# Two-layer graph attention on one core: the second weighing partly on ScalarE, and both low parts of the f32 turns at the head of VectorE's loop period

## The chip, the cores and the metric

The program runs on one core of a Trainium2 chip. The metric is the device time of one execution in microseconds (us), the median of several; lower is better. The profile is one execution recorded by the hardware profiler. Its engines are TensorE (PE, and PEld for its weight loads), VectorE (DVE), ScalarE (ACT), GpSimd (POOL) and SyncE (SP), which here only issues DMAs.

## The reference

Two graph-attention layers run over 4096 nodes with 128 features and one 4096 x 4096 adjacency matrix, f32 throughout:

```
h = relu(layernorm(x));  q, k, v = h@Wq.T+bq, h@Wk.T+bk, h@Wv.T+bv
x = x + elu(softmax(where(adj > 0, q@k.T/sqrt(128), -9e15)) @ v)          # layer 1
g = relu(layernorm(x));  t = g@W;  s1 = t@a[:128];  s2 = t@a[128:]
e = where(adj > 0, leaky_relu(s1[:,None] + s2[None,:], 0.01), -9e15)
x = x + t + softmax(e) @ g                                                # layer 2
```

## The kernel before

Both layers go through the nodes in 32 strips of 128 query rows. `T` is 32, `NC` is 8 chunks of four tiles of 128.

**Layer 1, the loop.** `all_periods` gives every engine 32 periods, one for each strip `s`; the middle 24 are a hardware loop of four periods a turn. The order on each engine is the order of the code, and engines meet only in counted semaphores. In period `s`:

- PE turns the last quarter of the exponentials of strip `s` in f32 (`turn`, i = 0 and 1), and in between computes scores of strips `s+1` and `s+2` (`make_scores`, 6 matmuls of 512 columns for each part `k` of 1024 columns). The rest is turned in bf16 (`turn_high`) and multiplied with v (`times_v`).
- ACT copies the two f32 turns out as bf16 high parts (`copy_pT`: tiles `pT_high0`, `pT_high1`), copies the next q strip, copies the sums and the bf16 turns (`copy_hiT`), takes the exponentials of strip `s+1` (`exps`, after the maximum of that strip) and ends with the elu of strip `s-1` (`elu_exp`).
- DVE makes the low parts of the f32 turns (`turned_low`, i = 0 and 1: f32 in PSUM minus the bf16 high part), the low parts of the exponentials in SBUF (`low_part`, k = 0, 1, 2), which SP then turns by DMA (`lowT`), adds the mask and takes the running maximum of strip `s+1` and `s+2` (`add_mask`, k = 0 to 3) and reduces it (`find_max`).
- POOL finishes the elu (`add_elu`, three small instructions), makes the additive mask of strip `s+2` (`make_mask`, L365, two halves), adds the halves of the sums (`add_halves`, two small ones) and turns the adjacency of strip `s+3` into bytes (`make_bytes`, L360, two halves).

`make_scores(s+2, 0)` overwrites the PSUM tile that `add_mask(s+1, 2)` reads, and so waits for it; `make_scores(s+2, 1)` waits for `add_mask(s+1, 3)` in the same way.

**The edge.** After the loop the rows are normalised, turned, and multiplied with `wa`. The features are weighed twice by exponentials of `s2`: `weigh(c)` writes `v1[0]`, and `weigh_words(c, 1)` writes `v1[1]`, chunk by chunk (L344). POOL splits each weighed chunk into two bf16 halves in place (`split_words`, L340). PE computes `t = g@W` with `hw_product(c)` in four PSUM tiles that `hw_add` empties. ACT writes sign bytes of strips 0 to 3 for each key tile (`sign_bytes`, L308; `EARLY` is strips 0 and 1, `LATE` strips 2 and 3). This block of code ends in a meeting of all five engines; each then loads a flag from memory (L1364) and branches to the fast way.

**Layer 2.** In the fast way DVE first computes exponents (L1437 to L1441), then weighs the chunks of `v1[1]` that are left, then makes the masks of strips 1, 2, 3 (`cut`, three instructions each: L323, L327, L332), then compares 12 key tiles for the next four strips, and then takes results and cuts by turns. PE sums strip after strip, 64 matmuls each (L1664): 32 key tiles with `v1[0]`, then 32 with `v1[1]`. In strip 0 each chunk of `v1[1]` beyond the early ones waits for POOL's split. Strip `s` waits for the mask `parts_ready` of `cut`. Four strips further the masks need the signs that ACT writes meanwhile.

`LOW_EARLY` is the number of chunks of `v1[1]` weighed ahead of the meeting, `LATE_EARLY` the number of key tiles whose `LATE` signs ACT writes ahead of it.

## Time and profile before

| | |
|---|---|
| median of three runs | 746.63 us (746.05 to 747.23) |
| the profiled execution | 748.01 us, of which its span 746.2 us |
| loop of layer 1, from the second f32 turn group to the last | about 78 to 451 us of the span |
| edge, from there to the first matmul of strip 1 in layer 2 | 451 to 516 us |
| layer 2 | 516 to 741 us, then the last result |
| busy share of the span | PE 96%, PEld 81%, DVE 76%, ACT 72%, POOL 61% |
| mean granted TensorE clock | 0.986 of full speed |

A timeline row gives the start in us of the span, the duration, the engine, the line, the operation and its tiles, the number of instructions merged into it, and in brackets the engine's idle time ahead of it with what ended it. Durations of neighbours on one engine overlap by some 0.1 us, so the distance between two starts is what an instruction costs. A windows row gives the stretch, its length, the busy time of each engine with its number of instructions, the granted clock, the DMA share and the GB/s. Spans on POOL are rough.

### The profile page before, as it was taken

Reading aid. Unit: us, or ns where it says so; the run is one execution under the profiler, and the core shown is the slowest. Engines: PE = TensorE matmul, PEld = TensorE weight load, DVE = VectorE, ACT = ScalarE, POOL = GpSimd, SP = SyncE. Lnnn points to the kernel's source line nnn. Section 1 sums busy time; section 2 is a strip of 40 time slices with the busy share of each in tenths; the row PEclk is TensorE's granted clock in tenths of the full one; section 3 lists DMA queues with packets and bytes.
Section 4 is the critical chain, followed back from the end, with each engine's and each line's share of the span. In section 5 each row is a group of like instructions: output and inputs, shape, how many; then the busy total and the mean of one; then the engine's idle time right before and its main releaser. Section 6 shows DMA issues by size and latency. Waiting matters only on the chain. (4 is left out here: it accounts for less than half of the span.)

```text
span 746.2 us, 18361 instructions
## 1 busy us (share of the span) xinstructions
PE 714.8 (96%) x6269; PEld 603.7 (81%) x6269; DVE 567.5 (76%) x1203; ACT 539.8 (72%) x1083; POOL 452.9 (61%) x388
## 2 busy tenths in 40 slices
PE   7988999999999999999999999967999999999997
PEld 5667888888888888888888878855888888888885
DVE  5977787787878878788787887779978477577572
ACT  4755877778777787777877778869597797887810
POOL 5688799999999999999999998664000000000000
PEclk9999999999999999999999999978999999999999
DMA  7179999998988989889798863994333343442200
GB/s 240 64 257 300 251 275 240 267 249 245 276 243 265 253 248 274 240 269 255 247 271 238 275 135 82 176 85 85 87 77 76 81 96 66 94 95 63 40 11 13
DMA packets 192784, 132.51 MB, mean 178 GB/s; under 512 B 173537, under 2 KB 180193, under 8 KB 184545
## 3 DMA queue, kind: packets, MB, share of 16 engines
q1 hardware_dynamic: 192000, 131.63, 66.4%
q8 instruction: 28, 0.46, 0.3%
q10 hardware_dynamic: 576, 0.26, 0.1%
q14 instruction: 20, 0.16, 0.1%
q0 software_dynamic: 160, 0.00, 0.0%
HBM read 71.04 MB, written 18.89 MB: 121 GB/s over the span
## 5 line engine op out<-in xcount | busy, mean ns | idle before, releaser
L797 ACT ACTIVATE scores<-scores,neg_max 128x1024 f32<-128x1024 f32 x128 | 146.1, 1143 | 45.3 <-DVE neg_max L928 45.3
L941 DVE TENSOR_TENSOR low<-scores 128x1024 bf16<-128x1024 f32 x96 | 135.6, 1412 | 38.5 <-ACT scores L797 38.4
L1210 PE MATMUL spare<-v_parts,hiT 128*128 128x256 bf16 x768 | 161.6, 274 | 0.0
L922 DVE CUSTOM_DVE_ANT_0 scores<-ps_s,mask_both 128x1024 f32<-128x1024 f32 x128 | 155.9, 1218 | 0.7 <-POOL mask_both L365 0.4
L365 POOL TENSOR_SCALAR mask_both<-mask_bytes 128x2048 bf16<-128x2048 uint8 x64 | 151.7, 2371 | 5.4 <-POOL mask_bytes L360 0.4
L360 POOL TENSOR_SCALAR mask_bytes<-adj_both 128x2048 uint8<-128x2048 int32 x64 | 148.5, 2338 | 3.8 <-DMA adj_both<-in_adj 3.0
L1206 PE MATMUL spare<-v_parts,lowT 128*128 128x128 bf16 x768 | 144.5, 220 | 4.3 <-DMA lowT<-low 4.3
L811 ACT ACTIVATE hiT<-spare 128x512 bf16<-128x512 bf16 (+1 forms) x128 | 102.5, 802 | 35.3 <-PE spare L1180 32.8
L1664 PE MATMUL ps_x<-q_parts,over_k 128*128 128x258 bf16 x1024 | 118.5, 276 | 5.5 <-POOL q_parts L340 2.5
L1664 PEld LDWEIGHTS ps_x<-q_parts,over_k 128*128 128x128 fp8e4 x1024 | 99.8, 99 | 22.7 <-POOL q_parts L340 3.3
L1145 PE MATMUL ps_s<-k_hi,q_strip 128*128 128x512 f32 x256 | 111.8, 437 | 2.4 <-PEq L83 1.9
L1146 PE MATMUL ps_s<-k_lo,q_strip 128*128 128x512 f32 x256 | 100.8, 394 | 0.0
L1147 PE MATMUL ps_s<-k_hi,q_strip 128*128 128x512 f32 x256 | 100.8, 394 | 0.0
L1210 PEld LDWEIGHTS spare<-v_parts,hiT 128*128 128x128 bf16 x768 | 75.5, 98 | 8.3
L1206 PEld LDWEIGHTS spare<-v_parts,lowT 128*128 128x128 bf16 x768 | 75.5, 98 | 7.6 <-issue 3.5
L308 ACT ACTIVATE v_parts<-s_block,s_col 128x512 fp8e4<-128x512 f32 x116 | 72.2, 717 | 0.0
L1592 ACT ACTIVATE sums<-ps_x,ac 128x258 f32<-128x258 f32 x63 | 26.3, 470 | 62.4 <-PE ps_x L1664 62.4
L1159 PE MATMUL spare<-ident,scores 128*128 128x128 f32 x256 | 69.4, 275 | 0.9 <-ACT hiT L811 0.9
L934 DVE TENSOR_TENSOR pT_low<-spare,pT_high 128x512 bf16<-128x512 f32 x64 | 43.9, 688 | 31.9 <-ACT pT_high L804 31.9
L1180 PEld LDWEIGHTS spare<-ident_half,scores 128*128 128x128 bf16 x768 | 46.3, 98 | 25.3 <-issue 23.8
L1180 PE MATMUL spare<-ident_half,scores 128*128 128x128 bf16 x768 | 64.8, 220 | 0.0
L1664 PE MATMUL ps_x<-q_parts,v_parts 128*128 128x258 bf16 x512 | 59.8, 273 | 0.0
(179 smaller groups left out, 1302.1 us busy)
## 6 DMA issues: line engine op xcount, KB each, us to landing
adj_both<-in_adj SPq DMA_DIRECT2D x64, 1024.0 KB, 5.3
mask_bytes_dram<-mask_bytes SPq DMA_DIRECT2D x32, 512.0 KB, 2.8
x_sb<-in_x SPq DMA_DIRECT2D x8, 256.0 KB, 8.4
out<-res SPq DMA_DIRECT2D x32, 64.0 KB, 1.6
lowT<-low SPq DMA_TRANSPOSE x96, 4.7
mask_both<-s_row_dram SPq DMA_DIRECT2D x2, 768.0 KB, 7.3
over_k<-mask_bytes_dram SPq DMA_TRANSPOSE x16, 4.6
scores<-mask_bytes_dram SPq DMA_TRANSPOSE x16, 4.6
```

The lines of the kernel that those rows point to most:

```text
L360: return nc.gpsimd.tensor_scalar(mask_bytes[par][:, half(h)], adj_sb[h], 1.0, 0.0, ALU.min, ALU.max)
L365: return nc.gpsimd.tensor_scalar(out, src, -NEG, NEG, ALU.mult, ALU.add)
L797: nc.scalar.activation(sc, sc, ACT.Exp, bias=neg_max[:, bn:bn + 1], accum_out=row_sum[:, bn, k:k + 1]).then_inc(exp_done, 1)
L811: nc.scalar.activation(hiT[k][:, half_of], ps_t[(2 + u) % 3][:].bitcast(BF16)[:, half_of], ACT.Copy).then_inc(hiT_ready, 1)
L922: nc.vector.tensor_tensor_reduce(out=scores[bn % 2][:, part(k)], in0=ps_s[k % 2][:], in1=mask[bn % 2][:, part(k)], scale=1.0, scalar=LOWES ...
L941: nc.vector.tensor_tensor(low[k][:], p, high_half(p), ALU.subtract).then_inc(low_done, 1)
L1145: nc.tensor.matmul(o, high, k_hi[:, col], start=True, stop=False)
L1146: nc.tensor.matmul(o, high, k_lo[:, col], start=False, stop=False)
L1180: last = nc.tensor.transpose(out[:, D * t:D * t + D], high[:, D * t:D * t + D], ident_half[:])
L1206: return nc.tensor.matmul(ps_a[:, 0, :], rest, v_parts[:, t, 0, :], start=False, stop=False)
L1210: last = nc.tensor.matmul(ps_a[:], high, v_parts[:, t, :, :], start=first, stop=final)
L1664: last = nc.tensor.matmul(ps_x[b % 2][k][:], by_key_tile(m, t)[:, b], v1[k][:, t, :].bitcast(BF16), start=(t == 0), stop=(t == T - 1))
```

## The change

In each loop period but the first and the last, `turned_low(s, 1)` stands right behind `turned_low(s, 0)`, ahead of `low_part(s, b, 1)` and `add_mask(s + 1, bn, 2)`. At the edge the chunks 2 to 5 of `v1[1]` are weighed by ACT ahead of the meeting, 16 activations of one tile each, and POOL splits them there, behind everything else that it does in this block. DVE weighs only chunks 0 and 1 ahead of the meeting, as before, and 6 and 7 behind it. ACT writes the `LATE` signs of 2 key tiles ahead of the meeting where it wrote 6, and of 22 behind it where it wrote 26; DVE writes those of the last 8 tiles between the masks of strips 1 and 2. PE computes `hw_product(4)` and `(5)` one place earlier each.

```diff
             EARLY = slice(0, 2)
             FIRST, MIDDLE, LAST = slice(0, 24), slice(24, 30), slice(30, 32)
-            LOW_EARLY = 2
+            LOW_EARLY = 6
+            LOW_VECTOR = 2
+            VECTOR_LATE = 8
             LATE = slice(2, 4)
-            LATE_EARLY = 6
+            LATE_EARLY = 2
...
                         if c == NC - 2:
-                            for n in range(LOW_EARLY):
+                            for n in range(LOW_VECTOR):
                                 pool.wait_ge(low_weighed, n + 1)
                                 split_words(pool, n, 1)
+                    for c in range(LOW_VECTOR, LOW_EARLY):
+                        pool.wait_ge(low_by_scalar, c - LOW_VECTOR + 1)
+                        split_words(pool, c, 1)
...
                     nc.scalar.activation(s1_row[:, 512:1024], ps_s3[1], ACT.Copy).then_inc(s1_out, 1)
+                    for c in range(LOW_VECTOR, LOW_EARLY):
+                        for t in range(4 * c, 4 * c + 4):
+                            last = nc.scalar.activation(v1[1][:, t, 0:D], h_sb[:, t, :], ACT.Relu, scale=v1[1][:, t, D:D + 1])
+                        last.then_inc(low_by_scalar, 1)
                     for t in range(LATE_EARLY):
                         sign_bytes(0, s1_row, t, LATE)
...
                             turned_low(s, 0)
+                            turned_low(s, 1)
                             low_part(s, b, 1)
                             add_mask(s + 1, bn, 2)
-                            turned_low(s, 1)
                             low_part(s, b, 2)
...
-                    for c in range(LOW_EARLY):
+                    for c in range(LOW_VECTOR):
                         weigh_words(c, 1).then_inc(low_weighed, 1)
...
                     s1_product(1, ps_s3[1])
+                    hw_product(4)
                     pe.wait_ge(top_ready, 1)
...
-                    hw_product(4)
+                    hw_product(5)
                     pe.wait_ge(top_d, 1)
...
-                    for c in range(5, NC):
+                    for c in range(6, NC):
                         hw_product(c)
...
                             if isinstance(g, int) and g == 0 and b == 2:
                                 dve.wait_ge(late_signs, 1)
+                                dve.wait_ge(vector_late, 1)
...
                         cut(0, 0, 1)
+                        for t in range(T - VECTOR_LATE, T):
+                            last = compare_bytes(nc.vector, 0, s1_row, t, LATE)
+                        last.then_inc(vector_late, 1)
                         cut(0, 0, 2)
...
-                        for t in range(LATE_EARLY, T):
+                        for t in range(LATE_EARLY, T - VECTOR_LATE):
                             last = sign_bytes(0, s1_row, t, LATE)
```

On DVE, in a period of the loop of layer 1: `pT_low0` and `pT_low1` are the low parts of the two f32 turns, `low1` and `low2` those of two parts of the exponentials, `scores1<-ps_s0` the masked scores. Before:

```order
L934 TENSOR_TENSOR pT_low0<-spare0,pT_high0 128x512
L941 TENSOR_TENSOR low1<-scores0 128x1024
L921 MEMSET gate 128x1
L922 ISA scores1,row_max<-ps_s0,mask_both 128x1024
L922 ISA row_max 128x1
L934 TENSOR_TENSOR pT_low1<-spare1,pT_high1 128x512
L941 TENSOR_TENSOR low2<-scores0 128x1024
```

And of the change, the same stretch:

```order
L943 TENSOR_TENSOR pT_low0<-spare0,pT_high0 128x512
L943 TENSOR_TENSOR pT_low1<-spare1,pT_high1 128x512
L950 TENSOR_TENSOR low1<-scores0 128x1024
L930 MEMSET gate 128x1
L931 ISA scores1,row_max<-ps_s0,mask_both 128x1024
L931 ISA row_max 128x1
L950 TENSOR_TENSOR low2<-scores0 128x1024
```

`low1` and the masked scores of part 2 now stand behind the second f32 turn; everything from `low2` on has its old place.

On DVE, behind the meeting, at the head of layer 2: `q_parts` is `v1[1]`, `over_k` the masks of strips 1 to 3, `v_parts` the next ones. Before:

```order
L344 SCALAR_TENSOR_TENSOR q_parts<-adj_both,q_parts 128x4x128 x6
L323 TENSOR_SCALAR over_k<-over_k 128x1024
L327 SCALAR_TENSOR_TENSOR over_k<-over_k 128x1024
L332 TENSOR_TENSOR over_k<-over_k 128x1024
L323 TENSOR_SCALAR over_k<-over_k 128x1024
```

And of the change:

```order
L344 SCALAR_TENSOR_TENSOR q_parts<-adj_both,q_parts 128x4x128 x2
L323 TENSOR_SCALAR over_k<-over_k 128x1024
L327 SCALAR_TENSOR_TENSOR over_k<-over_k 128x1024
L332 TENSOR_TENSOR over_k<-over_k 128x1024
L313 TENSOR_SCALAR over_k<-mask_both,s_col 128x2x128 x8
L323 TENSOR_SCALAR over_k<-over_k 128x1024
```

Four of six weighings are gone ahead of the mask of strip 1, and eight comparisons stand between it and the mask of strip 2.

On POOL, on both sides of the meeting (the branches and the load of the flag), where `q_parts` is split. Before:

```order
L340 TENSOR_TENSOR q_parts<-q_parts 128x516 x10
L573 UNCONDITIONAL_BRANCH
L1418 UNCONDITIONAL_BRANCH
L1364 TENSOR_LOAD flag
L1364 ISA x2
L1365 COMPARE_AND_BRANCH
L340 TENSOR_TENSOR q_parts<-q_parts 128x516 x6
```

And of the change:

```order
L340 TENSOR_TENSOR q_parts<-q_parts 128x516 x14
L575 UNCONDITIONAL_BRANCH
L1428 UNCONDITIONAL_BRANCH
L1374 TENSOR_LOAD flag
L1374 ISA x2
L1375 COMPARE_AND_BRANCH
L340 TENSOR_TENSOR q_parts<-q_parts 128x516 x2
```

Four splits have moved from behind the meeting to ahead of it.

## Rows read from the trace of the kernel before

**Rows 1.** Windows: the loop of layer 1.

```profile
78.47:451.30 372.83, 369.05 (x3362) 311.68 (x3361) 299.02 (x588) 283.57 (x561) 349.92 (x260) 1.00 0.87 249
```

**Rows 2.** Timeline of POOL, from one period's `add_halves` to the next one's.

```profile
313.69 0.46 POOL L710 TENSOR_TENSOR acc_sb<-acc_sb 128x128 f32<-128x128 f32 x1
...
321.24 5.64 POOL L365 TENSOR_SCALAR mask_both<-mask_bytes 128x2048 bf16<-128x2048 uint8 x2
...
326.96 0.46 POOL L710 TENSOR_TENSOR acc_sb<-acc_sb 128x128 f32<-128x128 f32 x1
```

**Rows 3.** Timeline of POOL in the period that begins at 438.19.

```profile
440.55 1.54 POOL L721 TENSOR_TENSOR x_sb<-x_sb,att_exp 128x128 f32<-128x128 f32 x1
442.17 4.73 POOL L365 TENSOR_SCALAR mask_both<-mask_bytes 128x2048 bf16<-128x2048 uint8 x2
```

**Rows 4.** Timeline of DVE: a low part beside rows 2, then the same period as rows 3.

```profile
320.79 1.44 DVE L941 TENSOR_TENSOR low<-scores 128x1024 bf16<-128x1024 f32 x1
...
440.56 1.22 DVE L941 TENSOR_TENSOR low<-scores 128x1024 bf16<-128x1024 f32 x1
...
443.44 1.70 DVE L941 TENSOR_TENSOR low<-scores 128x1024 bf16<-128x1024 f32 x1
...
446.33 0.16 DVE L928 TENSOR_REDUCE neg_max<-row_max 128x1 f32<-128x4 f32 x1
```

**Rows 5.** Timeline of ACT in the same period and the next.

```profile
438.89 0.30 ACT L825 ACTIVATE att_pos<-att 128x128 f32<-128x128 f32 x1
...
439.32 0.60 ACT L804 ACTIVATE pT_high<-spare 128x512 bf16<-128x512 f32 x1
...
441.82 0.60 ACT L804 ACTIVATE pT_high<-spare 128x512 bf16<-128x512 f32 x1 [1.50 <-PE spare L1159]
...
446.52 1.15 ACT L797 ACTIVATE scores<-scores,neg_max 128x1024 f32<-128x1024 f32 x1 [0.55 <-DVE neg_max L928]
...
452.62 0.58 ACT L804 ACTIVATE pT_high<-spare 128x512 bf16<-128x512 f32 x1
454.93 0.60 ACT L804 ACTIVATE pT_high<-spare 128x512 bf16<-128x512 f32 x1 [1.72 <-PE spare L1159]
```

**Rows 6.** Timeline of PE: first matmul of `make_scores(s+2, 0)` in that period.

```profile
445.32 0.48 PE L1145 MATMUL ps_s<-k_hi,q_strip 128*128 128x512 f32 x1
```

**Rows 7.** The chain that ended last, from the head of layer 2.

```profile
504.54 7.02 DVE q_parts L344 x6
...
516.31 52.22 PE ps_x L1664 x448
...
568.53 7.18 PE ps_x L1664 x64
```

**Rows 8.** Timeline of POOL: the last splits ahead of the meeting, and those behind it.

```profile
496.68 1.05 POOL L340 TENSOR_TENSOR q_parts<-q_parts 128x516 bf16<-128x516 f32 x1 [0.76 <-DVE q_parts L344]
505.22 8.70 POOL L340 TENSOR_TENSOR q_parts<-q_parts 128x516 bf16<-128x516 f32 x6 [7.49 <-DVE q_parts L344]
```

**Rows 9.** Timeline of PE at the edge.

```profile
489.70 0.39 PE L1269 MATMUL ps_s<-v_parts,ident_half 128*128 128x256 bf16 x1 [1.16 <-ACT scores L869]
...
499.01 3.40 PE L1280 MATMUL spare<-w_next,scores 128*128 128x128 f32 x24
503.81 5.54 PE L1664 MATMUL ps_x<-q_parts,over_k 128*128 128x258 bf16 x48 [1.40 <-issue]
```

**Rows 10.** Windows of 1 us at the edge; the clock is the third figure from the end.

```profile
489.00:490.00 1.00, 0.29 (x3) 0.30 (x4) 1.00 (x2) 1.00 (x8) 1.00 (x2) 0.87 1.27 288
...
520.00:521.00 1.00, 1.00 (x9) 0.80 (x8) 0.96 (x2) 1.00 (x2) 0.00 (x0) 0.77 0.00 0
```

**Rows 11.** Timeline of ACT: late signs ahead of the meeting and behind it.

```profile
495.07 2.57 ACT L308 ACTIVATE over_k<-mask_both,s_col 128x256 fp8e4<-128x256 f32 x6
504.86 10.49 ACT L308 ACTIVATE over_k<-mask_both,s_col 128x256 fp8e4<-128x256 f32 x26
```

**Rows 12.** Timeline of DVE: the twelve comparisons of layer 2.

```profile
522.48 4.84 DVE L313 TENSOR_SCALAR v_parts<-mask_both,s_col 128x512 uint8<-128x512 f32 x12
```

4 lines of the change are left out of this document (2 added, 2 removed).

## The prediction

> **What bounds the kernel now.** I read the profile in three steps: the windows of the loop, the timelines of the four engines within one of its periods, and then the chain that ended last with the timelines around the meeting.
>
> In the loop PE is busy for 369.05 of 372.83 us, and the clock is full [rows 1]. The stretch is 28 periods, so one takes 13.315 us on average. PE alone would need (369.05 / 28 =) 13.18, and what is missing, 3.78 us over all periods, is the most that any reordering in the loop can win. POOL explains most of it: from one `add_halves` to the next it takes (326.96 - 313.69 =) 13.27 us, with nothing but back-to-back work between [rows 2]. In that time it is held up once, by a `low_part` of DVE: the two halves of L365 take 5.64 us there [rows 2] and 4.73 in another period [rows 3]; in that other period it is the small L721 that starts with `low1` and takes 1.54 [rows 3, 4], where the small L710 takes 0.46 [rows 2]. So POOL loses 0.9 us or a little more to DVE in each period, and without that would need (13.27 - 0.91 =) 12.36.
>
> At the edge the chain runs through DVE. Behind the meeting it weighs six chunks in 7.02 us and makes the mask of strip 1, and only at 516.31 can PE begin strip 1 [rows 7]. From 516.31 on the chain is PE without a gap, at 7.18 us for 64 matmuls [rows 7]: layer 2 is bound by PE, and whatever moves the start of strip 1 moves the end. The first 448 matmuls take 52.22 us where 7 x 7.18 = 50.26 are normal, since the clock, which fell to half in the stalls of strip 0, is full again only in the window from 520 [rows 7, 10]. The effective start of a full-speed layer 2 is 516.31 + 1.96 = 518.27.
>
> **The loop.** No instruction is added or taken away. `pT_low1` moves ahead of `low1`, and since it needs ACT's second copy, DVE now waits for it before `low1`. In the period shown the first copy starts at 439.32, the second at 441.82 after an idle time of 1.50 [rows 5], so ACT could start it 1.00 after the first, and PE makes it wait. From the second copy `P` on I add up three cycles.
>
> First, ACT and DVE. Copy and its low part 1.24 (439.32 to 440.56, as for the first copy), of which `pT_low1` is about 0.6; `low1` and the mask of part 2 2.28 (440.56 to 443.44, less 0.60 for the `pT_low1` between); `low2` to the maximum 2.89 (443.44 to 446.33) [rows 4, 5]. `low2` takes 1.70 and `low1` 1.22 [rows 4], so 0.48 of the 2.89 is a wait, and 2.41 stays without it. Maximum to exponential 0.19, exponentials, copies and elu to the next first copy 6.10 (446.52 to 452.62), first copy to second 1.00 [rows 4, 5]. The sum is 1.24 + 2.28 + 2.41 + 0.19 + 6.10 + 1.00 = 13.22, or 13.70 with the wait.
>
> Second, PE and DVE. The mask of part 2 now ends at P + 1.24 + 2.28 = P + 3.52; in the period shown that is 445.34, and PE starts the scores that need it at 445.32 [rows 5, 6]. So this wait just closes. From there to the next second copy PE takes 454.93 - 445.32 = 9.61 [rows 5, 6]. The cycle is 13.13, and with an estimated 0.05 for the semaphore 13.18.
>
> Third, POOL: 12.36 if no low part holds it. `low1` will start at the first copy + 1.00 + 1.24 = + 2.24. The first half of L365 starts, without L721's hold of (1.54 - 0.46 =) 1.08, at 442.17 - 1.08 - 439.32 = + 1.77 [rows 2, 3, 5]. So `low1` comes 0.47 after it, which the trace doesn't show. Two cases bound it. L365 that starts 0.45 after a low part (321.24 against 320.79) costs POOL 0.91 and the low part 0.2 [rows 2, 4]. `low2` that starts 1.27 after L365 (443.44 against 442.17) is held 0.48 and POOL nothing [rows 3, 4]: the first half lets go 1.75 after its start, and the second half, which starts at 442.17 + 2.36 = 444.53 while `low2` still works until 445.06, isn't delayed, so that a half has no need of the port in its first 0.53 us. By that `low1` comes just in time to be first, by 0.06. It then holds POOL; if POOL becomes slower than the 13.22 of ACT by this, L365 slides later against `low1`, and the hold shrinks. I take POOL as held, with 13.27 as now, since the nearest case with POOL held costs what it loses now. The 28 periods then take what they take: **0 for the loop**, within -1.5 (28 x 0.05, period 13.22) and +2 us. The cover of this edit is thin: the mask of part 2 had ended some 2.5 us before PE needed it (443.44 - 0.60 against 445.32), and will end as it is needed.
>
> The Trainium skill, page "SBUF — State Buffer", section "Who interferes with whom", says that a VectorE instruction with two SBUF inputs and a GpSimd instruction that reads SBUF exclude each other, whichever starts first keeping the port pair for its whole length. Here the row differs: `low2`, which starts 1.10 before the end of the first L365 half, is held for 0.48 only [rows 3, 4]. By the page `low1` would be held for 2.36 - 0.47 = 1.9, and the rival below would be the likeliest case.
>
> **The edge, up to the meeting.** ACT's 16 activations cost 0.30 each at most [rows 5], 4.8 us from 495.07 on [rows 11], plus two signs at 2.57 / 6 = 0.43; it is done by 500.7 even so, and hidden by PE, which ends at 499.01 + 3.40 = 502.41 [rows 9]. PE has one product less at its end and fills a stall with it: some 1.1 us earlier, 501.3. POOL becomes the last. It ends now at 496.68 + 1.05 = 497.73, and gets four more splits. Each takes 1.05 alone and 8.70 / 6 = 1.45 beside DVE's weighing [rows 8]. That is 501.9 to 503.5, and since DVE works there on two instructions with two inputs of about the same length, I take 503.4. Behind the meeting PE starts 1.40 after the last engine's end [rows 9]: at **504.8**, 1.0 later than now.
>
> **The edge, behind it.** DVE starts weighing at 504.54 + 1.0 = 505.5, takes two chunks of 1.17 (7.02 / 6), and then as now 4.75 (511.56 to 516.31) for the mask of strip 1 [rows 7]: ready at 512.6 at the latest. PE's strip 0 no longer waits for splits: 504.8 + 7.2 = 512.0. But PE was idle from 501.3 to 504.8. An idle time of 1.40 at this meeting left the clock alone, one of 1.16 ahead of 489.70 was followed by its fall in the window from 489 [rows 9, 10]; 3.5 us will bring it down. It came back 4.2 us after PE's steady work began at 516.31, with a loss of 1.96 [rows 7, 10]. I take the same loss: strip 0 ends at 512.0 + 2.0 = 514.0, with its mask ready, and from there on the clock is full. The gain is 518.27 - 514.0 = **4.3 us**.
>
> What else moved is hidden. The eight comparisons cost less than 4.84 / 12 = 0.40 each [rows 12], 3.2 in all, up to 515.8; the 22 signs at 10.49 / 26 = 0.40 [rows 11] are done by 505.9 + 8.9 = 514.8; two more masks at most by 521. PE needs the mask of strip 2 at 521.2. ACT begins the next signs, those of strips 4 to 7, half a microsecond earlier than now (514.8 against 504.86 + 10.49 = 515.35 [rows 11]), and PE needs them 4.3 us earlier, at 514.0 + 3 x 7.18 = 535.5, 20.7 us after ACT begins; in the trace PE meets no wait there [rows 7], and I take it as hidden still. Were it not, at most (4.3 - 0.5 =) 3.8 us would come back.
>
> **The sum.** The profiled execution took 748.01 with a span of 746.2; the median of the runs is 746.63, 1.38 less. Against its own time: 748.01 + 0 - 4.3 = 743.7; against the median **742.3**.
>
> **The rivals.**
>
> *The edge gives more.* If POOL's splits aren't held (501.9) and PE's idle time is short enough to leave the clock alone, strip 1 begins when its mask is ready, at 503.3 + 0.7 + 2.34 + 4.75 = 511.1: a gain of 7.2. With the clock kept but POOL late it is 518.27 - 512.6 = 5.7. For it: one idle time of 1.40 without a fall. Against it: 2 to 3.5 us are longer than the one that did bring the fall. Time 739.4 to 740.9. Chance 0.15.
>
> *The gain is mostly eaten.* The clock stays low for 6 us in place of 4 (loss 3.0), the signs of strip 4 come late, or the loop costs 2 us more through masks that end just late. Gain of 0 to 1.5 against now, time 745.1 to 747. For it: the PE cycle in the loop has no slack left. Chance 0.15.
>
> *The slower side: `low1` queues behind L365.* It decides where `low1` starts more than 0.53 after L365, so 0.06 later than I worked out. Then it is held by up to 1.75 - 0.53 = 1.2, the mask of part 2 ends by so much later, and PE, which has no slack there, waits: 13.18 + 1.2 = 14.4 in such a period, 1.1 more than now. In all 28 that is 31 us; in a quarter to a half of them, since the phases of POOL and ACT shift against each other, 8 to 15. For it: the margin. Against it: POOL, when held, slides later, which puts `low1` first. Time with the edge's gain 750 to 765 (746.63 - 4.3 + 8 to 23), likeliest 752. Chance 0.25.
>
> **How the numbers follow.** The forecast, 742.3 with its own range of 740.8 to 745.1, has 0.45. The range reaches from 739.5 over the eaten gain to 752, into the slower case, and leaves out about two thirds of that, 0.17, and a little of the better edge, 0.2 in all. A difference of 0.2%, 1.5 us, is about what a measurement of this kernel tells from none. Faster by more: 0.45 + 0.15 = 0.60. Within: nearly all of the eaten gain, 0.13. Slower: 0.27.
>
> **What would show it.** In the loop: PE's busy share of the same 28 periods stays near 99%, the first scores matmul of strip s+2 begins within 0.1 us of the end of the mask of part 2, `low1` keeps 1.2 us, and POOL's L721 falls back to 0.46 while its L365 pair takes up to 5.6. If `low1` shows 2 us or more, the slower rival is it. At the edge: the last split ends at about 503.4 and PE's last product at 501.3; PE's first matmul of layer 2 follows 3.5 us later; one stretch of half clock of 3 to 6 us at the head of strip 0, and none at 513 to 520; no wait between strips 0 and 1. The prediction is wrong if any loop period is steadily above 13.4, or if layer 2 meets a later wait, for the signs of strip 4, which the sum takes as hidden.

## The result, and the profile after

| | before | after |
|---|---|---|
| median | 746.93 us (746.05 to 750.02, 4 runs) | 798.90 us (797.76 to 800.46, 4 runs) |
| ratio | | 1.0696 (1.0668 to 1.0724) |
| span of the profiled execution | 746.2 | 798.6 |
| one steady period of the loop | 13.29 | 15.19 |
| last maximum of the loop to the effective start of a full-speed strip 1 | 58.83 | 55.18 |

The change makes the kernel 7.0% slower. The difference of the two spans is 52.4 us, and it has two parts. The last `find_max` of the loop starts at 515.41 in place of 459.44, 56.0 us later. Of these, 2.1 are there at the first maximum (49.37 in place of 47.24), which in the traces of the other kernels comes anywhere from 45.6 to 49.6; the first two periods add 2.1, and the 28 behind them add 51.8, which is 1.90 in each steady one. The edge gives 3.65 back.

The page of the kernel after, costliest groups. The line numbers are those of the changed file: L950 is `low_part`, L931 `add_mask`, L1154 the first matmul of a part of the scores, L802 the exponentials. At the end of a row stands the idle time ahead of the group and what ended it.

```profile
L802 ACT ACTIVATE scores<-scores,neg_max 128x1024 f32<-128x1024 f32 x128 | 146.1, 1143 | 127.3 <-DVE neg_max L937 127.3
L950 DVE TENSOR_TENSOR low<-scores 128x1024 bf16<-128x1024 f32 x96 | 170.9, 1780 | 41.8 <-ACT scores L802 41.6
L1154 PE MATMUL ps_s<-k_hi,q_strip 128*128 128x512 f32 x256 | 113.4, 443 | 42.7 <-DVE row_max L931 40.2
```

No instruction of these was added, so nothing but durations and waits can explain the time. `low` takes 1780 ns on average (1412 before), PE waits 40.2 us for the mask of part 2, and the list of waits gives 93.3 us in which POOL waits for ACT's elu. Before, POOL worked back to back [rows 2] and PE was at 99% of the loop [rows 1]. Over 426 us of the new loop PE is busy for 90.5% (a windows row: stretch, length, busy time of each engine, granted clock):

```profile
80.00:506.00 426.00, 385.65 (x3374) 319.90 (x3372) 337.15 (x590) 281.80 (x563) 321.18 (x262) 0.98 0.83 220
```

Now one period of the kernel after, by timeline. First POOL, then DVE, then PE:

```profile
326.74 0.45 POOL L720 TENSOR_TENSOR att_exp<-att_exp,ones 128x128 f32<-128x128 f32 x1 [3.10 <-ACT att_exp L832]
328.47 4.73 POOL L365 TENSOR_SCALAR mask_both<-mask_bytes 128x2048 bf16<-128x2048 uint8 x2
...
328.05 0.69 DVE L943 TENSOR_TENSOR pT_low<-spare,pT_high 128x512 bf16<-128x512 f32 x1 [0.19 <-ACT pT_high L809]
328.66 2.78 DVE L950 TENSOR_TENSOR low<-scores 128x1024 bf16<-128x1024 f32 x1
331.37 1.22 DVE L931 CUSTOM_DVE_ANT_0 scores<-ps_s,mask_both 128x1024 f32<-128x1024 f32 x1
332.52 1.75 DVE L950 TENSOR_TENSOR low<-scores 128x1024 bf16<-128x1024 f32 x1
...
332.65 0.50 PE L1154 MATMUL ps_s<-k_hi,q_strip 128*128 128x512 f32 x1 [1.78 <-DVE row_max L931]
```

The reader is to see three starts. L365 starts at 328.47, `low1` 0.19 us later, and `low1` takes 2.78 where it alone takes 1.22 [rows 4]. It is held for 1.56: it gets to work at 328.66 + 1.56 = 330.22, 1.75 us after the start of L365. PE then begins its scores 0.06 after the mask of part 2 has ended (331.37 + 1.22), having waited 1.78. `add_mask` (L931) reads one operand from PSUM and one from SBUF, `low_part` both from SBUF; the mask of part 2 works beside the same L365 and keeps its 1.22.

The same engines one period earlier, where PE made its second turn late, and ACT copied it late (POOL, DVE, and a windows row of PE some 10 us before):

```profile
313.27 4.73 POOL L365 TENSOR_SCALAR mask_both<-mask_bytes 128x2048 bf16<-128x2048 uint8 x2
318.08 1.31 POOL L712 TENSOR_TENSOR acc_sb<-acc_sb 128x128 f32<-128x128 f32 x1
319.89 3.75 POOL L360 TENSOR_SCALAR mask_bytes<-adj_both 128x2048 uint8<-128x2048 int32 x2
...
314.86 1.39 DVE L950 TENSOR_TENSOR low<-scores 128x1024 bf16<-128x1024 f32 x1
316.18 1.21 DVE L931 CUSTOM_DVE_ANT_0 scores<-ps_s,mask_both 128x1024 f32<-128x1024 f32 x1
317.32 1.75 DVE L950 TENSOR_TENSOR low<-scores 128x1024 bf16<-128x1024 f32 x1
320.26 0.16 DVE L937 TENSOR_REDUCE neg_max<-row_max 128x1 f32<-128x4 f32 x1
...
304.00:306.00 2.00, 2.00 (x15) 1.63 (x15) 1.77 (x5) 0.73 (x1) 1.92 (x3) 0.50 0.40 78
```

Here `low1` starts 1.59 after L365 and is held for 0.17, to 315.03: again 1.76 after L365's start. The mask of part 2 starts 2.91 after L365 here and 2.90 there. So the period doesn't depend on when `low1` is ready; it hangs on L365. The cycle closes: L365 to the maximum 6.99 (313.27 to 320.26), maximum to exponentials 0.20, exponentials and elu until POOL starts 6.28 (320.46 to 326.74), the three small instructions of POOL until L365 1.73. The sum is 15.20, the period.

Over 28 periods `low1` is held for 1.45 to 1.57 in 17, for 1.2 to 1.3 in 5, and for 0.13 to 0.22 in the 6 where it starts some 1.6 after L365; each time it gets to work 1.75 after L365's start. In the loop the granted clock is at half six times, for instance from 303.3 to 306.7, behind PE's wait for the mask, and each of the six late `low1` follows one of these. The period is 15.19 with and without, so the low clock isn't what makes it long.

The row of L360 shows what was misread ahead of the run. Two halves that nobody holds take 3.75. The L365 pair of 4.73 [rows 3] was therefore held already. The trace of the kernel before has its halves one by one:

```profile
442.17 1.90 POOL L365 TENSOR_SCALAR mask_both<-mask_bytes 128x2048 bf16<-128x2048 uint8 x1
444.15 2.75 POOL L365 TENSOR_SCALAR mask_both<-mask_bytes 128x2048 bf16<-128x2048 uint8 x1
```

The second half waited 0.85 for `low2`, which had started at 443.44.

The edge, by the timeline of the kernel after:

```profile
552.35 7.10 POOL L340 TENSOR_TENSOR q_parts<-q_parts 128x516 bf16<-128x516 f32 x5 [0.76 <-DVE q_parts L344]
...
554.01 2.94 PE L1289 MATMUL spare<-w_next,scores 128*128 128x128 f32 x16
560.99 12.24 PE L1678 MATMUL ps_x<-q_parts,over_k 128*128 128x258 bf16 x86 [4.03 <-issue]
...
566.28 1.23 DVE L332 TENSOR_TENSOR over_k<-over_k 128x1024 uint32<-128x1024 uint32 x1
567.43 2.19 DVE L313 TENSOR_SCALAR over_k<-mask_both,s_col 128x256 uint8<-128x256 f32 x8
570.86 1.23 DVE L327 SCALAR_TENSOR_TENSOR over_k<-over_k 128x1024 uint32<-128x1024 uint32 x1 [0.65 <-ACT over_k L308]
```

POOL is the last engine at the meeting, at 559.45; PE had ended at 556.95 and starts layer 2 at 560.99. The mask of strip 1 is ready at 567.5. Windows of the same place, and the chain of work that ended last:

```profile
557.00:559.00 2.00, 0.00 (x0) 0.00 (x0) 0.00 (x0) 0.00 (x0) 2.00 (x3) 1.00 0.00 0
559.00:561.00 2.00, 0.01 (x1) 0.02 (x2) 0.19 (x1) 0.00 (x0) 0.45 (x1) 0.58 0.00 0
561.00:563.00 2.00, 2.00 (x10) 1.42 (x11) 1.93 (x7) 1.32 (x4) 0.71 (x1) 0.50 0.69 28
563.00:565.00 2.00, 2.00 (x11) 1.40 (x10) 1.97 (x2) 2.00 (x6) 2.00 (x2) 0.50 0.86 48
565.00:567.00 2.00, 2.00 (x15) 1.53 (x13) 1.97 (x2) 2.00 (x6) 0.17 (x1) 0.71 0.51 55
```

```profile
560.99 59.86 PE ps_x L1678 x512
620.86 7.18 PE ps_x L1678 x64
```

The clock is at half (1.2 GHz) from 559.3 to 566.2. Eight strips take 59.86 where 8 x 7.18 = 57.44 are normal, a loss of 2.42, and there is no other gap: the chain runs through strips 0 and 1 without a wait for a mask.

### The profile page after: what moved, and what is told of

It is laid out like the page before. It is cut to its first block and busy times, and to the rows that moved or that the text cites. A ratio compares the mean times of both kernels' runs of the same rounds, so it can differ in the third digit from the quotient of the medians.

```text
span 798.6 us, 18373 instructions
## 1 busy us (share of the span) xinstructions
PE 730.9 (92%) x6269; PEld 612.3 (77%) x6269; DVE 601.5 (75%) x1207; ACT 537.7 (67%) x1091; POOL 423.0 (53%) x388
## 5 line engine op out<-in xcount | busy, mean ns | idle before, releaser
L802 ACT ACTIVATE scores<-scores,neg_max 128x1024 f32<-128x1024 f32 x128 | 146.1, 1143 | 127.3 <-DVE neg_max L937 127.3
L950 DVE TENSOR_TENSOR low<-scores 128x1024 bf16<-128x1024 f32 x96 | 170.9, 1780 | 41.8 <-ACT scores L802 41.6
L1219 PE MATMUL spare<-v_parts,hiT 128*128 128x256 bf16 x768 | 166.1, 280 | 0.0
L931 DVE CUSTOM_DVE_ANT_0 scores<-ps_s,mask_both 128x1024 f32<-128x1024 f32 x128 | 155.7, 1217 | 0.0
L1215 PE MATMUL spare<-v_parts,lowT 128*128 128x128 bf16 x768 | 149.3, 224 | 3.5 <-DMA lowT<-low 3.5
L1154 PE MATMUL ps_s<-k_hi,q_strip 128*128 128x512 f32 x256 | 113.4, 443 | 42.7 <-DVE row_max L931 40.2
L365 POOL TENSOR_SCALAR mask_both<-mask_bytes 128x2048 bf16<-128x2048 uint8 x64 | 146.0, 2282 | 5.4 <-POOL mask_bytes L360 0.4
L360 POOL TENSOR_SCALAR mask_bytes<-adj_both 128x2048 uint8<-128x2048 int32 x64 | 122.0, 1924 | 6.2 <-DMA adj_both<-in_adj 5.3
L1156 PE MATMUL ps_s<-k_hi,q_strip 128*128 128x512 f32 x256 | 103.0, 402 | 0.0
L1155 PE MATMUL ps_s<-k_lo,q_strip 128*128 128x512 f32 x256 | 102.6, 401 | 0.0
L1154 PEld LDWEIGHTS ps_s<-k_hi,q_strip 128*128 128x128 f32 x256 | 48.8, 191 | 56.7 <-DVE row_max L931 39.8
L1219 PEld LDWEIGHTS spare<-v_parts,hiT 128*128 128x128 bf16 x768 | 77.2, 101 | 9.8
L1215 PEld LDWEIGHTS spare<-v_parts,lowT 128*128 128x128 bf16 x768 | 77.5, 101 | 6.5 <-ACT hiT L816 3.1
```

The lines of the kernel that those rows point to most:

```text
L360: return nc.gpsimd.tensor_scalar(mask_bytes[par][:, half(h)], adj_sb[h], 1.0, 0.0, ALU.min, ALU.max)
L365: return nc.gpsimd.tensor_scalar(out, src, -NEG, NEG, ALU.mult, ALU.add)
L802: nc.scalar.activation(sc, sc, ACT.Exp, bias=neg_max[:, bn:bn + 1], accum_out=row_sum[:, bn, k:k + 1]).then_inc(exp_done, 1)
L931: nc.vector.tensor_tensor_reduce(out=scores[bn % 2][:, part(k)], in0=ps_s[k % 2][:], in1=mask[bn % 2][:, part(k)], scale=1.0, scalar=LOWES ...
L950: nc.vector.tensor_tensor(low[k][:], p, high_half(p), ALU.subtract).then_inc(low_done, 1)
L1154: nc.tensor.matmul(o, high, k_hi[:, col], start=True, stop=False)
```

## The experiments

Times beside "before" are ratios to the kernel before on the same chip, with their intervals. Fourteen kernels ran. "Period" is the steady one; in some kernels every fourth is longer by some 0.25, and a few early ones by more. L365, `low0`, `low1`, `low2` are named as above, whatever the line is in a kernel's own file. "Held" is the time of a `low` beyond the 1.22 that it takes alone.

### The loop's edit alone, and the edge's alone

`e1_loop_only` is the kernel before with only the swap:

```diff
                             turned_low(s, 0)
+                            turned_low(s, 1)
                             low_part(s, b, 1)
                             add_mask(s + 1, bn, 2)
-                            turned_low(s, 1)
```

> The kernel before with nothing but the new order of the two low parts in the loop. Port theory (GpSimd's mask instruction starts first, keeps the shared port 1.75 us, and VectorE's low part of the exponentials queues behind it in every period) and order theory (VectorE's wait for ScalarE's second copy is what costs, the port adds little) both put the whole loss here: 799 to 804 us, period 15.2 us, since the edge should have won 3 to 4 us in the full change. If the edge carries part of the loss, this is below 798.

Measured: 800.97 us, ratio 1.0710 (1.0690 to 1.0729), period 15.19, PE's wait for the mask of part 2 38.9 us. `e2_edge_only` is the kernel after with the old order in the loop:

```diff
                             turned_low(s, 0)
-                            turned_low(s, 1)
                             low_part(s, b, 1)
                             add_mask(s + 1, bn, 2)
+                            turned_low(s, 1)
```

> The full change with the loop in its old order. By my sum for the edge (a gain of 4.3 us; the trace of the full change suggests 3.7) the time is 742.3 to 743.5 us and the loop period 13.3. If the edge is a loss or gains nothing, 746 or more.

Measured: 743.15 us, ratio 0.9934 (0.9914 to 0.9954), period 13.29. The whole loss is the swap, and the edge is a gain. From the last maximum (459.79) to the effective start of strip 1 (505.82 + 58.96 - 7 x 7.18 = 514.52) it takes 54.73, where it took 58.83.

```profile
505.82 58.96 PE ps_x L1678 x512
```

### Is it POOL's reading of the mask bytes, or the order by itself?

`e3_mask_unread` is `e1_loop_only` with a mask that POOL writes without reading anything. It leaves out the masking of layer 1.

```diff
-                return nc.gpsimd.tensor_scalar(out, src, -NEG, NEG, ALU.mult, ALU.add)
+                return nc.gpsimd.memset(out, 0.0)
```

> The new order in the loop, but GpSimd fills the additive mask with zeros by a memset and reads no SBUF for it; this leaves out the masking of layer 1. Port theory: VectorE's low1 takes 1.2 us in place of 2.8, the period falls to 13.1 to 13.4 us, the time to 742 to 750. Order theory: low1 may be short, but the period stays above 14.2 us and the time above 770, because the wait for the second copy is still there.

Measured: 752.71 us, ratio 1.0063 (1.0040 to 1.0086), period 13.38; `low1` and the period are as the port theory had them, the time is 2.7 above its range. Timeline of POOL, then DVE, and a windows row of 20 periods:

```profile
298.34 3.55 POOL L365 MEMSET mask_both<- 128x2048 bf16 x2
...
298.97 1.22 DVE L941 TENSOR_TENSOR low<-scores 128x1024 bf16<-128x1024 f32 x1
301.26 1.22 DVE L941 TENSOR_TENSOR low<-scores 128x1024 bf16<-128x1024 f32 x1
...
170.00:437.56 267.56, 267.15 (x2396) 222.78 (x2394) 205.35 (x421) 202.01 (x400) 198.86 (x181) 1.00 0.95 255
```

`low1` starts 0.63 behind L365 and works beside it for all of its 1.22. So 48 of the 53 us that the swap costs are POOL's read of SBUF against the two SBUF inputs of `low_part`. The remaining 5 us are the price of the new order with a mask that isn't read: 0.09 in each steady period makes half of it, and the other half lies among the early periods of this trace, where two take 14.42 and 14.82. The old order with an unread mask wasn't run, so what the order alone costs isn't shown. The windows row says what bounds this loop: PE is busy for 267.15 of 267.56 us. That `low1` works beside a memset unheld agrees with the Trainium skill, page "SBUF — State Buffer", section "Who interferes with whom", which has the contention only with a GpSimd instruction that reads SBUF, not with one that only writes it.

### The mask ahead of the elu in POOL's period

`e4_mask_first` is `e1_loop_only` with `make_mask` ahead of `add_elu`; `e5_mask_first_old` is `e2_edge_only` with the same move, so with DVE's old order.

```diff
+                        if has(c, b, 2):
+                            make_mask(*at(c, b, 2))
                         if has(c, b, -2):
                             add_elu(s - 2)
-                        if has(c, b, 2):
-                            make_mask(*at(c, b, 2))
```

> The new order in the loop, and GpSimd makes the mask ahead of the three elu instructions in each period, so that it starts when the bytes are done and not when ScalarE's elu is. Port theory: the mask pair is then mostly over when low1 starts, low1 waits less than 0.6 us, and the period falls to 13.2 to 13.8 us: 745 to 762. Order theory: period 15.2 as in the run with the loop edit alone, 800.

Measured: 777.73 us, ratio 1.0401 (1.0381 to 1.0422), period 14.27, every fourth 14.52. The expected 745 to 762 was missed: less than half of the loss is back. Timeline of POOL, then DVE:

```profile
305.11 3.88 POOL L365 TENSOR_SCALAR mask_both<-mask_bytes 128x2048 bf16<-128x2048 uint8 x2 [0.36 <-POOL mask_bytes L360]
...
307.36 2.70 DVE L941 TENSOR_TENSOR low<-scores 128x1024 bf16<-128x1024 f32 x1 [1.23 <-ACT scores L797]
```

`low1` is nearly free (1.44), but `low0` now stands behind L365's second half for 1.48, and `low2` behind L360 for 0.96 (2.18).

> The edge of the change with the loop order of before, and in POOL's period make_mask ahead of add_elu. It is the control of the kernel that had the new order and the mask first: 777.7 us, a period of 14.3 to 14.5. Port theory (a low part of DVE and a half of POOL's mask exclude each other, whoever starts first keeps the port, POOL for 1.75 of the 1.90 us of a half): the first half starts with the end of ACT's elu, 1.2 us before low1, so low1 is held about 0.5 us, which is hidden because the mask of part 2 has 2.5 us of cover in the old order; low2 meets the second half and is held by up to 1.2. Period 13.3 to 13.9, total 743 to 760, clearly under 777.7. Rival (the place of the mask on POOL itself costs the loop, whatever DVE's order is): 14.3 and 771 or more.

Measured: four runs of 743.15, 766.23, 766.84 and 768.53 us. The profile is of the last. In it the period is 14.17 from the fifth period to the 28th, `low0` 2.70 and `low2` 2.11, and POOL waits 1.67 for ACT in each period. So the same program came out at two times 23 us apart. The mean granted clock doesn't tell them apart (0.990 in the quick run, 0.986, 0.989 and 0.993 in the others). That the quick run kept another pattern of starts through the loop is inferred from its time alone, since it has no profile. The expected range held the one time and missed the other; the rival's 771 was not reached either. What decides between them is open, and this control settles nothing about `e4_mask_first`.

### Smaller pieces of the mask

`e6_mask_quarters` is `e1_loop_only` with each half of L365 as two instructions of 1024 columns:

```diff
+                for piece in range(2):
+                    cols = slice(N // 2 * h + N // 4 * piece, N // 2 * h + N // 4 * piece + N // 4)
...
+                    last = nc.gpsimd.tensor_scalar(out, src, -NEG, NEG, ALU.mult, ALU.add)
+                return last
```

> Only the new loop order (801.0 us by itself, period 15.19, low1 2.5 to 2.8), and POOL makes each half of the mask as two instructions of 1024 columns. Port theory: the port is handed over at the end of an instruction, so low1 waits 0.85 in place of 1.75 us after L365's start, and the cycle that sets the period gets 0.9 shorter: period 14.2 to 14.4, total 768 to 778, low1 under 2.1 us. Rival A (POOL's whole pass over the mask slows DVE, whatever the pieces): no change, 800. Rival B (the new order itself is what costs): no change, 800.

Measured: 788.73 us, ratio 1.0521 (1.0483 to 1.0558), period 14.60. Timeline:

```profile
304.11 6.12 POOL L367 TENSOR_SCALAR mask_both<-mask_bytes 128x1024 bf16<-128x1024 uint8 x4
...
304.29 1.93 DVE L944 TENSOR_TENSOR low<-scores 128x1024 bf16<-128x1024 f32 x1
```

`low1` is held for 0.71 where it was held for 1.56; it gets the port 0.89 after the start of the first piece, as the theory had it. The total was missed by over 10 us: the third piece catches `low2` (2.02, where it was 1.75), so that the period is 14.60 and not 14.2 to 14.4, and two periods of this trace took 15.84 and 17.46. `low0` meets L360 (2.41), which by the table of holds below costs the period nothing. `e9_quarters_old`, the same split on `e2_edge_only`:

> The edge of the change with the loop order of before, and each half of POOL's mask made as two instructions of 1024 columns. The control by itself takes 743.2 us with a period of 13.29, of which PE's own work is 13.18. Port theory: with the new order the split took 12 us off, since low1 was held 0.7 in place of 1.6. In the old order low1 starts ahead of L365 and low2 behind it; smaller pieces hold low2 less at the first piece but can catch it again at the next, and a piece costs POOL 1.5 in place of 1.9 for a half, so POOL's own work grows by 2.2 us to 12.7 in a period and with two holds of 0.9 passes 13.3. Expected 743 to 756, likeliest 747. Rival (smaller pieces are better in any order): 740 to 743, period under 13.25.

Measured: 753.38 us, ratio 1.0061 (1.0038 to 1.0083), period 13.55, within the expectation. One of its eight runs took 2565 us, for a reason that isn't known; the ratio is of the other seven. In the old order the split costs some 10 us against `e2_edge_only`: `low2` is up from 1.70 to 1.96, `low0` from 1.41 to 1.67.

### Who starts first

Three kernels with the new order move the start of L365 against `low1`. In `e7_mask_after_low1` POOL waits for the end of `low1`; in `e8_mask_with_low1` the same line waits for `(pT_low_ready, 2 * s - 2)`, the second `pT_low`, behind which DVE starts `low1` at once. In `e14_mask_behind_halves` no wait is added (second piece of the diff).

```diff
+                        if not (isinstance(s, int) and s < 2):
+                            pool.wait_ge(low_done, 3 * s - 4)
+                            pool.sem_inc(pool_gate, 1)
```

```diff
+                        if has(c, b, -1):
+                            add_halves(s - 1)
                         if has(c, b, 2):
                             make_mask(*at(c, b, 2))
-                        if has(c, b, -1):
-                            add_halves(s - 1)
```

> Only the new loop order, and POOL's mask of strip s+2 waits for the end of low1 of strip s, so that low1 never stands behind it. Port theory: low1 is back at 1.22 us; low2 starts about 1.1 us behind the first half and is held 0.6 to 0.7 (1.9 us); POOL starts its mask later but has 1.5 us of slack. Period 13.5 to 14.1, total 755 to 773. Rival (the order itself, through PE's wait for the mask of part 2, costs, and not the port): 15 and more than 790, since POOL's work is only made later.

Measured: 773.54 us, ratio 1.0340 (1.0286 to 1.0394), period 13.96, every fourth 14.21. `low1` is at 1.22. The period is within the expectation, the time half a microsecond above it.

```profile
299.76 4.73 POOL L365 TENSOR_SCALAR mask_both<-mask_bytes 128x2048 bf16<-128x2048 uint8 x2 [1.67 <-DVE low L944]
...
300.63 2.10 DVE L944 TENSOR_TENSOR low<-scores 128x1024 bf16<-128x1024 f32 x1
```

`low2` starts 0.87 behind L365 and is held for 0.88, until 1.75 after its start: the same number as for `low1` above.

> Only the new loop order, and POOL's mask of strip s+2 waits for the low part of the second f32 turn, behind which DVE starts low1 at once. If the first to start keeps the port whole, DVE's next instruction is there before POOL has woken: low1 1.2 to 1.45 us, the first half of L365 is held by it and lasts 2.8 to 3.1, low2 is held by 0.5 or less; period 13.4 to 13.8, total 752 to 765. If POOL wins such a race instead: low1 2.9, period 15 and 795. If both share the port evenly: low1 about 2, period 14.1, total 770.

Measured: 765.27 us, ratio 1.0230 (1.0195 to 1.0265), period 13.62, every other one 13.75 to 13.88, within the expectation, the time 0.3 above it. Timeline of DVE, then POOL:

```profile
305.16 1.22 DVE L944 TENSOR_TENSOR low<-scores 128x1024 bf16<-128x1024 f32 x1
307.45 1.76 DVE L944 TENSOR_TENSOR low<-scores 128x1024 bf16<-128x1024 f32 x1
...
305.44 5.52 POOL L365 TENSOR_SCALAR mask_both<-mask_bytes 128x2048 bf16<-128x2048 uint8 x2 [0.70 <-DVE pT_low L937]
```

This is the direct test: L365 starts 0.28 after `low1`, and it is L365 that pays (5.52 for the pair, the first half alone 2.69 in place of 1.90), while `low1` keeps its 1.22 in every period. In the kernel after it was 0.19 the other way round, and `low1` took 2.78. Evenly shared, both would have been near 2.

> Only the new loop order, and in POOL's period add_halves stands ahead of make_mask. No wait is added: the sums that add_halves needs are copied by ACT behind its second f32 copy, when low1 is about to start, so that POOL's mask starts behind low1 by itself. If who starts first decides: low1 is back at 1.2 us with nobody told to wait, the small add_halves takes some of the hold (1.2 in place of 0.46), low2 is held 0.5 to 1.0 by the mask; period 13.5 to 13.9, total 755 to 768. If instead DVE loses whenever POOL has mask work pending: low1 over 2 us and 780 or more.

Measured: 784.13 us, ratio 1.0465 (1.0438 to 1.0492), period 14.40, every fourth 14.65. Timeline of POOL, then DVE:

```profile
301.41 4.73 POOL L365 TENSOR_SCALAR mask_both<-mask_bytes 128x2048 bf16<-128x2048 uint8 x2
306.22 3.75 POOL L360 TENSOR_SCALAR mask_bytes<-adj_both 128x2048 uint8<-128x2048 int32 x2
...
302.09 2.29 DVE L941 TENSOR_TENSOR low<-scores 128x1024 bf16<-128x1024 f32 x1
308.75 2.30 DVE L941 TENSOR_TENSOR low<-scores 128x1024 bf16<-128x1024 f32 x1 [1.23 <-ACT scores L797]
```

`low1` is at 1.43 with nobody told to wait, so the start does decide. But the total was missed by 16 us: `low2` now is held for 1.07, until 1.75 after the start of L365, and `low0` for 1.08. I had given `low2` 0.5 to 1.0 and `low0` nothing. The 0.21 of `low1` goes to the small L710, which starts 0.10 ahead of it.

### The edge

All four are `e2_edge_only` with one edit. `e10_low_early4` and `e12_low_early5` weigh fewer chunks ahead of the meeting (`LOW_EARLY` 4 and 5 in place of 6):

```diff
-            LOW_EARLY = 6
+            LOW_EARLY = 5
```

`e11_busy_meeting` and `e13_busy_short` give PE f32 products of 512 columns that nobody reads, 12 and 3 of them, ahead of the meeting:

```diff
+                    pe.wait_ge(hT_ready, NP2)
+                    for _ in range(12):
+                        nc.tensor.matmul(turned_x[0], wa_rep[:], hT2[:, 0:512], start=True, stop=True)
```

> The edge of the change with the loop order of before (743.2 us by itself), with 4 chunks weighed ahead of the meeting in place of 6: ACT weighs two fewer, and POOL, the last engine at the meeting (504.1 against PE's own end 2.5 us earlier), ends 2.8 us earlier. Theory of the edge as the profile after has it (POOL's last split sets the meeting, PE idles 4 us, the clock falls and costs 2.4): the meeting is 2.5 earlier, no fall of the clock, but DVE weighs four chunks behind it for 4.7 in place of 1.3, so that the mask of strip 1 comes 0.8 later than now: total 741 to 743.5. Rival (ACT's 16 activations or something else sets the meeting): unchanged meeting, mask later by 3.4, total 745 to 747.

> The edge of the change with the loop order of before (743.2 us by itself), with 5 chunks weighed ahead of the meeting. POOL ends 1.4 us earlier, so the meeting is 1.4 earlier; DVE weighs three chunks behind it, one more, for 1.2. The mask of strip 1 comes at about the same time, 0.2 earlier, and PE's strip 0 starts 1.4 earlier and is through, low clock included, before or as the mask is ready. Total 741.8 to 743. Rival (POOL doesn't set the meeting): 744.4 or more.

> The edge of the change with the loop order of before (743.2 us by itself), and PE makes 12 products of 512 columns that nobody reads, behind its last one ahead of the meeting, some 2.6 us, so that it stands idle for 1.5 to 2.8 us at the meeting in place of 4 to 5.3. If the idle time is what brings the clock down: the clock stays full through strip 0, and the 2.4 us come back: 740.5 to 741.3. If PE becomes the last engine at the meeting by mistake: up to 1 us later. Rival (the clock falls at the meeting whatever PE did ahead of it): 743.2 unchanged, the clock at half for the same 4 us.

> The edge of the change with the loop order of before (743.2 us by itself), and PE makes 3 f32 products of 512 columns that nobody reads behind its last one ahead of the meeting. The kernel with 12 of them showed 0.87 us each and a full clock behind the meeting, but its meeting came 8 us late. Three take 2.6 and end with POOL's last split, so the meeting stays in place and PE stands idle for about 1.5 us in place of 4 to 5.3. If the idle time brings the clock down, strip 0 runs at full clock and 2.4 us come back: 740.8. Rival (what helped there was the length of steady work, and 2.6 us more of it don't do): 743.2 and a half clock behind the meeting.

| kernel | median, ratio | PE idle at the meeting | 512 matmuls or strip 0 | edge |
|---|---|---|---|---|
| `e2_edge_only` | 743.15, 0.9934 (0.9914 to 0.9954) | 5.31 | 58.96 | 54.73 |
| `e10_low_early4` | 742.70, 0.9937 (0.9915 to 0.9959) | 2.99 | strip 0: 8.57 | 53.22 |
| `e12_low_early5` | 741.62, 0.9926 (0.9900 to 0.9951) | 2.88 | strip 0: 7.32 | 52.90 |
| `e11_busy_meeting` | 750.70, 1.0037 (1.0018 to 1.0056) | 1.34 | 57.40 | 60.42 |
| `e13_busy_short` | 744.25, 0.9919 (0.9895 to 0.9943) | 2.43 | 58.86 | 54.36 |

"Edge" is again the time from the start of the last maximum to the effective start of strip 1 in the profiled run. The ratios of four of them (all but `e11`) don't tell them apart; the traces do, within one execution each. The time of `e10` is as expected (741 to 743.5), that of `e12` is 0.2 under its 741.8 to 743, and the expectations of `e11` and `e13` failed.

`e10` and `e12` confirm that POOL's last split sets the meeting. From the last maximum to PE's start of layer 2 it is 46.03 with 6 chunks, 45.01 with 5 and 43.57 with 4. With 4, DVE's weighing of the other four behind the meeting takes that back: PE waits 1.07 for the mask of strip 1. The other half of `e10`'s expectation was wrong: the clock fell there too (half from 502.2 to 505.6), and strip 0 took 8.57 in place of 7.18. At 5 chunks the clock was full at the head of layer 2 and PE waited only 0.56 for the mask of strip 1:

```profile
503.02 7.32 PE L1678 MATMUL ps_x<-q_parts,over_k 128*128 128x258 bf16 x64 [2.88 <-issue]
510.91 1.29 PE L1678 MATMUL ps_x<-q_parts,over_k 128*128 128x258 bf16 x10 [0.56 <-DVE over_k L332]
```

`e11` kept the clock, but I had taken a product as 0.22 and it took 0.87, so PE itself came 8 us late to the meeting (timeline, then the chain):

```profile
501.72 10.47 PE L1325 MATMUL ps_s<-scores,wa_rep 128*128 128x512 f32 x24
513.53 57.40 PE ps_x L1681 x512
```

`e13` has the meeting in place and PE idle for 2.43; the clock still fell, and 58.86 - 57.44 = 1.42 were lost, so its expectation of 740.8 failed. Idle times of 1.34 lost nothing, of 2.43 lost 1.42, of 4.03 lost 2.42 in the kernel after; but 5.31 lost 1.52, 2.99 (`e10`) lost 1.39 and 2.88 (`e12`) nothing. The idle time at the meeting may be part of the cause; it doesn't settle the size, nor whether there is a loss at all. In `e12` the clock had been down ahead of the meeting and had just come back (windows; the granted clock is the third number from the end of a row):

```profile
490.00:495.00 5.00, 4.16 (x12) 2.83 (x13) 4.96 (x8) 5.00 (x17) 4.49 (x4) 0.50 1.27 73
495.00:500.00 5.00, 5.00 (x28) 4.71 (x27) 3.78 (x8) 3.10 (x10) 4.75 (x3) 0.63 1.20 0
502.00:504.00 2.00, 0.98 (x9) 0.87 (x10) 1.23 (x5) 0.43 (x2) 0.00 (x0) 1.00 0.11 8
```

In the others of this table it had been down ahead of the meeting as well, but was back earlier (at 495.5 in `e2`, 495.3 in `e10`, 496.4 in `e13`, 498.7 in `e12`). Whether that is why it stayed full stays open. `e12_low_early5` has the lowest time of this study, 0.7% ahead of the kernel before; by its ratio `e13_busy_short`, measured beside other runs of the kernel before, is level with it (0.9926 and 0.9919).

### The holds, added up

| kernel with the new order | held: low1 | low2 | steady period | period less the two |
|---|---|---|---|---|
| `e8_mask_with_low1` | 0 | 0.54 | 13.62 | 13.08 |
| `e7_mask_after_low1` | 0 | 0.88 | 13.96 | 13.08 |
| `e14_mask_behind_halves` | 0.21 | 1.07 | 14.40 | 13.12 |
| `e6_mask_quarters` | 0.71 | 0.80 | 14.60 | 13.09 |
| after | 1.56 | 0.53 | 15.19 | 13.10 |

Five kernels leave the same 13.1, and `e4_mask_first`, with 14.27 - 0.22 - 0.96 = 13.09, fits as well. So in the new order both holds lie on the cycle of DVE and ACT (in the kernel after by way of POOL's small elu steps), microsecond for microsecond. The row of the kernel after is for the periods with the full hold; where `low1` comes late by itself, its lateness takes the place of the hold. `low0` isn't on the cycle: it is held for 0.06 in the kernel after, 0.2 in `e7` and `e8`, 1.08 in `e14`, 1.19 in `e6` and 1.48 in `e4`, and 13.1 is left each time. Nor is POOL's own work (three small elu steps 1.7, the halves 1.0, L365 and L360 some 3.9 each by starts, together 10.5) the bound. With no hold at all (`e3_mask_unread`) the period is 13.38 and PE is busy all the time, so PE takes over there; why its work then takes 13.36 in each period, and 13.18 before [rows 1], isn't shown.

## Why the prediction was wrong

The forecast was 742.3, the result 798.9, outside the range of 739.5 to 752. By its own steps:

**What bounds the kernel.** PE in the loop and DVE at the edge: right. "POOL loses 0.9 us or a little more to DVE in each period" was wrong: it loses 0.9 three times. The L721 that takes 1.54 [rows 3] or the L365 pair at 5.64 [rows 2] show one, the second half of the L365 pair another (2.75 against 1.90 unheld), the second half of the L360 pair a third (2.87 against 1.90). POOL's own work is 10.5, not 12.36, and with the three holds, 2.8 together, that is the 13.27 of [rows 2].

**The loop: this step failed.** The step is that the second half "isn't delayed, so that a half has no need of the port in its first 0.53 us", from which `low1` "comes just in time to be first, by 0.06". It came from splitting 4.73 into two equal halves of 2.36. The halves are 1.90 and 2.75: the first ends earlier, the second is held by `low2`. With that split no free time of half a microsecond at the head of an instruction is left. A second row was misread with it: the 0.2 us that `low1` loses in rows 4 isn't lost to L365, which starts 0.45 behind it, but to L721, which starts 0.10 ahead of it (320.69 against 320.79). The positions were nearly right: `low1` was to start 0.47 after L365 and started 0.19 after it. By the forecast's rule that made `low1` first with more to spare; it was held for 1.56, and PE waited for it. The ordering rule of the forecast is replaced by what `e8`, `e7` and the kernel after show: whoever starts first keeps the port, and POOL keeps it for 1.75 of the 1.90 of a half. That is the rule of the Trainium skill, page "SBUF — State Buffer", section "Who interferes with whom", which I had set aside because a row seemed to differ; it differed only as long as two merged instructions were read as equal. The measured hold ends 0.15 before the whole length.

**The three cycles.** ACT and DVE without a hold: 13.22 forecast, 13.10 by the table. PE: 13.18, and in `e3` the period is 13.38. The sums were good; what they lacked is the hold, 1.56 for `low1` and 0.53 for `low2`, 2.09 together, where the forecast had named 0.48 and left it out of its 13.22.

**The slower rival.** Its place, its sign (`low1` of 2 us and more) and its mechanism are what happened, with a chance of 0.25. Its price was 8 to 23 us, and the swap cost 53 (`e1_loop_only`). The hold was priced as 1.2 and is 1.56, and a period with it as 1.1 longer and is 1.90 longer; the larger error is the share of periods, a quarter to a half, "since the phases of POOL and ACT shift against each other". It is all of them. POOL's L365 comes 1.8 after the end of ACT's elu and `low1` 1.2 after ACT's next copies: once POOL waits for ACT (3.10 in every period), both hang on the same engine, and only a late second turn of PE changes the distance, which leaves the period as it is. "POOL, when held, slides later", the argument against the rival, needs a first half of L365 that is held; here only the second half is (2.75), and POOL then waits for ACT anyway.

**The edge, up to the meeting.** Counted from the last maximum, PE's last product was to end at 41.9 and ended at 41.5, POOL's last split at 44.0 and 44.0, PE's start at 45.4 and 45.6. Right. The four moved splits took 6.05 where 5.7 was taken, and began 0.3 earlier, so the exact 44.0 is in part luck.

**The edge, behind it.** The mask of strip 1 was ready 1.1 earlier than forecast (52.1 against 53.2 after the last maximum) and not the bound. The loss by the low clock was taken as 2.0 and was 2.42. Gain forecast 4.3, measured 3.65; mechanism right, size 0.65 off. In `e2_edge_only`, whose edge has the same code, the clock cost 1.52 and the gain was 4.10. The comparisons took 0.27 each, under the 0.40, and no wait for the signs of strip 4 shows in the chain.

**The sum in its place.** 746.6 + 51.8 in the 28 periods + 4.2 ahead of them - 3.65 = 799.0, against 798.9 measured. The terms are read from the two traces, so this shows where the time went and is no second forecast; 2.1 of the 4.2 stand in the first maximum, which comes at other times in other runs.

## What to carry to other kernels

Where VectorE reads two SBUF tiles while GpSimd reads one, work out for each such pair which instruction starts first, and charge the later one with the whole rest of the other; a few tenths of a microsecond in a start are then worth an instruction's length in every period, and a wait that is taken away at one pair turns up at the next. Before a duration is taken as unheld, look at a row of a single instruction: a merged row hides a hold. And when an engine stops being saturated it becomes tied to the engine that it waits for, so that the phases between them can become fixed, as they did here, for better or worse.

## What the runs showed of the hardware

- Of two such instructions the one that starts first holds the other until about 0.15 us before its own end. A GpSimd instruction of 1.90 us (2048 columns, bytes to bf16) lets a waiting `low` to work 1.75 after its start (`low1` 0.19 and 1.59 behind it in the kernel after, `low2` 0.68 in `e14` and 0.87 in `e7`), one of 1.04 us (1024 columns, `e6`) after 0.89, one of 0.46 after 0.32 (L721 before, at 320.69). The other way round it is 1.07 of the 1.22 of a `low` (`e8`: L365 starts 0.28 behind it and is held for 0.79). Whether the port is free before the end, or the waiting instruction does without it at its head, these rows can't tell. Nor do they order a tie: L721 at 440.55 was the one held, by `low1` at 440.56 [rows 3, 4].
- A GpSimd `memset` of the same tile (3.55 for two halves) holds nobody: `low1` 1.22 beside it (`e3_mask_unread`). Nor does L365 hold an `add_mask`, which reads one operand from PSUM: 1.22 beside it in the kernel after.
- One program took 743.2 us in one run and 766.2 to 768.5 in three, with no difference in its code or data, nor one in its granted clock that goes with it (`e5_mask_first_old`).
- The low clock behind an idle time isn't a function of that idle time alone: 2.43 us (`e13`) and 2.99 (`e10`) brought it, and 2.88 (`e12`) didn't.
